# A transformer block's setup reordered: transfers in another order, filler matmuls, some work moved between engines

## The chip, the core and the metric

One core of a Trainium2 chip runs the whole program. Its engines are named as in the profile: PE (TensorE: matmuls, and PEld its weight loads), DVE (VectorE), ACT (ScalarE), POOL (GpSimd), SP (SyncE, which only issues transfers here). The metric is the device time of one execution in microseconds (us); lower is better. Everything stays in float32: a product in which accuracy matters is made of three matmuls on a high and a low part of each operand (names ending in _hi and _lo).

## What is computed

Eight sequences of 256 tokens with 256 features pass an attention block and a mixture-of-experts block, both modulated by a condition vector per sequence:

```python
mod = (silu(c) @ wmod).reshape(8, 6, 1, 256)
sa, ca, ga, sb, cb, gb = (mod[:, i] for i in range(6))
ga, gb = bounded(ga), bounded(gb)        # sign kept, size at least 0.25
h = layernorm(x) * (1 + ca) + sa
x = x + ga * attention(h, W_pack, W_o, conv_k, conv_v)
h = layernorm(x) * (1 + cb) + sb
x = x + gb * experts(h)                  # 32 experts, top 4, and a shared one
```

attention: qkv = h @ W_pack gives 16 query heads and 8 key and value heads of 128 features; q and k are rotated (x * cos + swapped x * sin), k and v pass a causal convolution of two taps per head; scores have a causal window of 128; the heads' outputs go through W_o.

## The kernel before

**Tiles and stages.** The batch is worked in four pairs of sequences (512 tokens). For a pair, h is held transposed (features on partitions) in two chunks c of 128 features, each as hT_hi and hT_lo. A projection project(m) makes one head of 128 features for the 512 tokens: six matmuls of 512 columns into one of two PSUM banks PJ (two chunks times hi*hi, hi*lo, lo*hi). The heads of a group come as k, q, v, q (head_of). 128 steps n of attention units follow (32 a pair), each with scores, softmax, a transpose of the probabilities, the weighted values and the output product; projections run four steps ahead (LEAD), so a prologue of four steps does project(0) to project(3) and nothing else. After the 128 steps come the shared expert and the 32 experts.

**Order.** It is written out by hand: each engine has its own program, `for n in STEPS` with the same step numbers, and the engines meet in semaphores. Hooks in the first pair's steps do further setup: W_STEPS and WO_STEPS split the later weight chunks and W_o into hi and lo parts (w_high, wo_high on ACT; w_low, wo_low on DVE a step later), MOD_STEPS compute the rest of the modulation.

**The setup, engine by engine.** SP (lines 343 to 373) issues in this order: c, ident, the first pair's rows xin (512 KB, line 347), the first third of the modulation weights wm (512 KB, line 349), the eight chunks wraw of W_pack (512 KB each, line 352, in W_ORDER), W_o as one transfer (2,048 KB, line 359), the rest of wm (1,024 KB), and next_x(1), the second pair's rows, which waits for the first pair's transposes (line 365); then the router's weights and the clearing of slot_rows. ACT (from line 482) issues cosT and sinT, computes silu(c) (L488), then issues mask, tri, ebase, wnorm, cwk and cwv (L494): eight small tables that share the semaphore ld_const.

PE (from line 1328): waits for silu and ident, transposes silu(c) (L1342) into bank U0, waits for DVE's copy scT and for wm, and computes the four 128-feature pieces of scale and shift with 16 matmul instructions of 8 columns (L1348) into U1. It then waits for modT and transposes the normalised rows (L1357, four a chunk, into U0 and U1). DVE: statistics of xin as soon as it has landed (L934, L937), the normalisation in place (L945), modT (L919, L920), the lo parts of weight chunks 0 and 1 (w_low, L1007), then hT_lo of both chunks (L951), then w_low of the third. ACT: rstd (L499, L500), w_high of chunks 0 and 1 (L578), then for each c the scaling hst (prepare_h, L508, two operations) and hT_hi (prepare_hi, L515), then w_high of the third. Weight chunks beyond these three (W_FIRST) are split in W_STEPS.

**Rotation of a projected head** (project and rope): ACT copies the halves swapped from PJ into qsw (L532, L533), DVE multiplies PJ by cosT (L965), POOL multiplies qsw by sinT (L768) and adds (L772); rope_done counts the sums. Then for k: ACT's tap (L540) and DVE's convolution kc (L970). The first scores (L1387, L1388) need kc and the first rotated q.

The waits that the change touches: ACT, DVE and POOL wait for all eight tables before their first steps, PE before step 0; PE waits for W_o before step 3; project(0) waits for both h_lo_done and, as every projection of the first pair, for w_lo_done.

```python
pe.wait_ge(modt_done, 1)          # before the transposes, line 1351
...
if l == 0:
    pe.wait_ge(h_lo_done, HC * (p + 1))
...
if p == 0:
    pe.wait_ge(w_lo_done, w_chunks(l))
```

## Time and profile before

| what | value |
|---|---|
| median of 3 runs | 765.53 us (765.27 to 766.3) |
| the profiled execution | 769.37 us, its span 766.9 us |
| PE / DVE / ACT / POOL busy | 731.1 / 531.6 / 467.7 / 425.5 us |
| mean granted PE clock | 0.990 |
| transferred | 84.42 MB, mean 110 GB/s |

Busy time is the sum over an engine's instructions; the span runs from the first to the last of them, and the execution's own time lies 2.5 us above it. The page divides the span into 40 slices of 19 us. In the first, PE is busy three tenths and in the second eight; from the fourth to the twenty-seventh it is busy nine tenths or more. Transfers are at eight to nine tenths of their engines in the first two slices and then mostly low.

### The profile page before, as it was taken

What the parts mean: (1) busy time and instruction counts of PE and PEld (TensorE: products, weight loads), DVE (VectorE), ACT (ScalarE), POOL (GpSimd) and SP (SyncE); (2) the same over time, 40 slices, a digit from 0 to 9 for tenths busy, and PEclk for the clock granted to TensorE, in tenths of its full rate; (3) what the DMA queues carried; (4) which work ended last, traced back from release to release, by engine and by line L of the source; (5) the groups of instructions that cost most, each with busy time, mean ns of one, the idle gap of its engine ahead of it and who ended that gap; (6) DMA issues with size and microseconds to landing.
All of it is one profiled execution on the core that took longest, in us unless ns stands there. A gap on an engine that the chain in (4) does not pass through costs nothing.

```text
span 766.9 us, 12813 instructions
## 1 busy us (share of the span) xinstructions
PE 731.1 (95%) x4114; PEld 620.8 (81%) x4114; DVE 531.6 (69%) x1552; ACT 467.7 (61%) x1277; POOL 425.5 (55%) x337
## 2 busy tenths in 40 slices
PE   3899999999999999999999999999988999999997
PEld 3688889998899898889989888989866767777775
DVE  4598788679877768987776797778665215564373
ACT  5688878777886677788667777877554212222110
POOL 0644445554466488646647875654534517468356
PEclk9999999999999999999999999999999999999999
DMA  8960005800005011100401101040359689996772
GB/s 294 322 136 1 2 1 175 287 1 2 1 1 168 26 40 48 40 1 1 158 8 40 46 28 62 16 165 1 123 145 237 191 289 272 282 240 74 163 233 82
DMA packets 62353, 84.42 MB, mean 110 GB/s; under 512 B 6312, under 2 KB 50229, under 8 KB 62288
## 3 DMA queue, kind: packets, MB, share of 16 engines
q1 hardware_dynamic: 51440, 70.56, 29.8%
q0 software_dynamic: 7680, 8.95, 6.2%
q10 hardware_dynamic: 3168, 4.11, 1.5%
q8 instruction: 33, 0.54, 0.3%
q14 instruction: 32, 0.26, 0.1%
HBM read 54.81 MB, written 33.51 MB: 115 GB/s over the span
## 4 chain that ended last, share of the span: by engine, by line
PE 76%; DVE 11%; ACT 6%; DMA 2%; issue 2%; POOL 1%; SPq 0%; ACTq 0%; POOLq 0%
PE PJ L1335 22%; PE OUT L1443 9%; PE U L1428 6%; PE U L1388 6%; PE U L1593 5%; PE U L1417 4%; PE U L1387 3%; PE U L1429 3%; PE U L1335 3%; PE OUT L1539 3%; PE U L1539 2%; PE XB L1612 2%; PE OUT L1612 2%; PE XB L1335 2%; ACT U L546 1%
## 5 line engine op out<-in xcount | busy, mean ns | idle before, releaser
L768 POOL TENSOR_TENSOR qsw<-qsw,sinT 128x512 f32<-128x512 f32 x96 | 126.2, 1314 | 184.6 <-ACT qsw L533 183.7
L977 DVE CUSTOM_DVE_ANT_0 U<-U,mask 128x128 f32<-128x128 f32 (+1 forms) x256 | 86.6, 379 | 54.8 <-PE U L1388 54.4
L546 ACT ACTIVATE U<-U,nmax 128x128 f32<-128x128 f32 (+1 forms) x256 | 100.4, 392 | 32.2 <-DVE nmax L977 31.7
L1335 PE MATMUL PJ<-hT_hi,w_hi 128*128 128x512 f32 x256 | 113.8, 445 | 4.0 <-DVE hT_lo L951 3.7
L1335 PE MATMUL PJ<-hT_lo,w_hi 128*128 128x512 f32 x256 | 103.5, 404 | 0.0
L1335 PE MATMUL PJ<-hT_hi,w_lo 128*128 128x512 f32 x256 | 103.1, 403 | 0.0
L772 POOL TENSOR_TENSOR qr<-qr,qsw 128x512 f32<-128x512 f32 x64 | 82.5, 1289 | 31.3 <-DVE qr L965 30.8
L532 ACT ACTIVATE qsw<-PJ 64x512 f32<-64x512 f32 x96 | 57.0, 594 | 58.1 <-PE PJ L1335 49.3
L779 POOL DMA_INDIRECT slot_rows<-xn,sidx x64 | 64.4, 1006 | 45.6 <-issue 12.0
L1443 PE MATMUL OUT<-wo_hi,oT_hi 128*128 128x256 f32 x256 | 83.0, 324 | 1.4 <-DVE wo_lo L1001 1.2
L994 DVE TENSOR_TENSOR oT_lo<-U,oT_hi 128x256 fp32r<-128x256 f32 x128 | 54.1, 423 | 41.2 <-ACT oT_hi L553 41.0
L1428 PE MATMUL U<-pT,vN 128*128 128x256 f32 x256 | 77.7, 385 | 1.8 <-ACT pT L566 1.1
L1388 PE MATMUL U<-kc,qr 128*128 128x256 f32 x256 | 77.4, 385 | 0.0
L987 DVE TENSOR_TENSOR prob<-U,rinv 128x384 f32<-128x384 f32 x128 | 71.4, 558 | 4.4
L1443 PE MATMUL OUT<-wo_hi,oT_lo 128*128 128x256 f32 x256 | 72.7, 284 | 0.0
L553 ACT ACTIVATE oT_hi<-U 128x256 fp32r<-128x256 f32 x128 | 49.3, 385 | 38.0 <-PE U L1429 30.8
L862 POOL DMA_INDIRECT expert_sum<-ye,slot_token x32 | 49.7, 1552 | 39.6 <-DVE ye L1276 23.2
L1443 PE MATMUL OUT<-wo_lo,oT_hi 128*128 128x256 f32 x256 | 71.6, 280 | 0.0
L1387 PEld LDWEIGHTS U<-kc,qr 128*128 128x128 f32 x256 | 47.5, 192 | 25.2 <-DVE oT_lo L994 7.9
L566 ACT ACTIVATE pT<-U 128x384 f32<-128x384 f32 x128 | 63.3, 495 | 0.7 <-PE U L1417 0.7
L1417 PE MATMUL U<-ident,prob 128*128 128x128 f32 x384 | 63.0, 273 | 0.2 <-DVE prob L987 0.2
L1335 PEld LDWEIGHTS PJ<-hT_hi,w_hi 128*128 128x128 f32 x256 | 49.5, 193 | 13.2 <-DVE hT_lo L951 4.1
(212 smaller groups left out, 1827.6 us busy)
## 6 DMA issues: line engine op xcount, KB each, us to landing
wgu<-in_dram SPq DMA_DIRECT2D x32, 352.0 KB, 9.4
expert_sum<-blank SPq DMA_DIRECT2D x3, 2176.0 KB, 17.8
slot_rows<-blank SPq DMA_DIRECT2D x1, 4624.0 KB, 26.3
late_sums<-expert_sum SPq DMA_DIRECT2D x9, 512.0 KB, 8.9
wd_a<-in_dram SPq DMA_DIRECT2D x12, 352.0 KB
wraw<-in_dram SPq DMA_DIRECT2D x8, 512.0 KB, 11.5
bcm<-mod_rows SPq DMA_DIRECT2D x8, 512.0 KB, 6.8
xe<-slot_rows ACTq DMA_DIRECT2D x10, 289.0 KB, 6.3
```

The lines of the kernel that those rows point to most:

```text
L546: last = act.activation(U[n % 3][:, a:z], U[n % 3][:, a:z], ACT.Exp, scale=-1.0, bias=nmax[:, n % 4, j:j + 1], accum_out=rsum[:, n % 4, j: ...
L768: pool.tensor_tensor(pair3(qsw[:, n % NQSW, :]), pair3(qsw[:, n % NQSW, :]), both(sinT[:, :]), ALU.mult).then_inc(t2_done, 1)
L772: pool.tensor_tensor(rope_buffer(m), rope_buffer(m), qsw[:, n % NQSW, :], ALU.add).then_inc(rope_done, 1)
L779: pool.indirect_dma_start(out=slots_d, out_offset=bass.IndirectOffsetOnAxis(ap=sidx[:, c:c + 1], axis=0), in_=xn[:, p % 2, c // TOPK, :], ...
L977: last = dve.tensor_tensor_reduce(out=U[n % 3][:, a:z], in0=U[n % 3][:, a:z], in1=allowed, scale=-float(HD) ** -0.5, scalar=3.4e38, op0=AL ...
L987: dve.tensor_tensor(prob[:, n % 2, :].rearrange("p (j k) -> p j k", k=PN), U[n % 3][:, 0:3 * PN].rearrange("p (j k) -> p j k", k=PN), rinv ...
L1335: last = pe.matmul(out_ap, a(c), b_(c), start=(n == 0), stop=(n == len(steps) - 1))
L1387: pe.matmul(U[n % 3][:, 0:PN], q[:, 0:PN], k[:, 0:PN], start=True, stop=True)
L1388: pe.matmul(U[n % 3][:, PN:3 * PN], q[:, PN:S], k, start=True, stop=True).then_inc(sc_ps, 1)
L1417: last = pe.transpose(U[n % 3][:, j * PN:(j + 1) * PN], prob[:, n % 2, j * PN:(j + 1) * PN], ident[:, :])
L1428: pe.matmul(o, v[:, 0:PN], pT[:, n % 2, 0:S], start=True, stop=False)
L1443: last = pe.matmul(OUT[b][:, t * H:(t + 1) * H], o, w[:, head, :], start=(head == 0 and t == 0 and i == 0), stop=(head == NH - 1 and i == ...
```

## The change

One commit changes the setup and nothing behind the first pair's steps:

- **Transfers.** ident and the first third of wm move to the head of ACT's queue. The first rows come in two halves, each with its own semaphore. The eight tables move from ACT's queue to SP's: cosT, sinT, cwk and cwv (semaphore ld_rope) behind the third weight chunk; mask, tri, ebase and wnorm (ld_const) behind the fourth. W_o comes in four parts: part 0 behind these, part 1 behind the second pair's rows, parts 2 and 3 behind the last chunk. The second pair's rows come behind the seventh chunk; the rest of wm comes last.
- **PE.** Fifteen filler matmuls (spin: ident by ident into OUT0, whose content is never read): 3 before the transposes of silu(c), 2 behind them, 5 behind the wm matmuls, 5 behind the transposes of x. The transposes no longer wait for modT, since the small products now lie in XB and U2. Head 0 has an order of its own: first the products with hT_hi of both chunks, then those with hT_lo.
- **Between engines.** The scaling of chunk 1 goes from ACT to DVE (first_h), the lo parts of the first two weight chunks from DVE to POOL, and the sine product and sum of head 0 from POOL to DVE. On ACT hT_hi of chunk 1 comes right behind that of chunk 0.
- **Waits.** Each engine waits for ld_rope before its first steps and for ld_const where the mask (DVE, step 0) or tri (PE, step 32) is first read; ACT waits for the part of W_o that it splits; ht_used counts one less.

The diff, cut:

```diff
@@ sync
-            sp.dma_start(ident[:, :], ident_t).then_inc(ld_ident, 16)
-            sp.dma_start(xin[:, :, :], x_pair(0)).then_inc(ld_xin, 16)
             wm_src = wmod.rearrange("(c p) n -> p c n", p=PN)
-            sp.dma_start(wm[:, :, 0:2 * H], wm_src[:, :, 0:2 * H]).then_inc(ld_wm, 16)
+            for b in range(2):
+                sp.dma_start(xin[:, 2 * b:2 * b + 2, :],
+                             x[b * S:(b + 1) * S, :].rearrange("(t p) h -> p t h", p=PN)).then_inc(ld_first[b], 16)
...
             for j in W_ORDER[:W_FIRST]:
                 w_load(j)
-            for j in W_ORDER[W_FIRST:]:
-                w_load(j)
-            sp.dma_start(wo[:, :, :], w_o.rearrange("(n p) h -> p n h", p=PN)).then_inc(ld_wo, 16)
-            sp.dma_start(wm[:, :, 2 * H:6 * H], wm_src[:, :, 2 * H:6 * H]).then_inc(ld_wmr, 16)
+            for dst, src in ((cosT[:, :], cos_t), (sinT[:, :], sin_t),
+                             (cwk[:, :], conv_k.rearrange("g t -> (g t)").partition_broadcast(PN)),
+                             (cwv[:, :], conv_v.rearrange("g t -> (g t)").partition_broadcast(PN))):
+                sp.dma_start(dst, src).then_inc(ld_rope, 16)
+            w_load(W_ORDER[W_FIRST])
+            for dst, src in ((mask[:, :], mask_t[:, PN:3 * PN]), (tri[:, :], tri_t), (ebase[:, :], ebase_t),
+                             (wnorm[:, :], w_norm.partition_broadcast(PN))):
+                sp.dma_start(dst, src).then_inc(ld_const, 16)
...
+            wo_load(0)
+            for j in W_ORDER[W_FIRST + 1:W_FIRST + 4]:
+                w_load(j)
             next_x(1)
+            wo_load(1)
+            w_load(W_ORDER[W_FIRST + 4])
+            wo_load(2)
+            wo_load(3)
+            sp.dma_start(wm[:, :, 2 * H:6 * H], wm_src[:, :, 2 * H:6 * H]).then_inc(ld_wmr, 16)
@@ scalar
-            act.dma_start(cosT[:, :], cos_t).then_inc(ld_const, 16)
-            act.dma_start(sinT[:, :], sin_t).then_inc(ld_const, 16)
+            act.dma_start(ident[:, :], ident_t).then_inc(ld_ident, 16)
+            act.dma_start(wm[:, :, 0:2 * H], wmod.rearrange("(c p) n -> p c n", p=PN)[:, :, 0:2 * H]).then_inc(ld_wm, 16)
...
-            for c in range(HC):
-                prepare_h(0, c, U[c])
-                prepare_hi(0, c)
+            prepare_h(0, 0, U[0])
+            prepare_hi(0, 0)
+            prepare_hi(0, 1)
             w_high(W_FIRST - 1)
...
-            act.wait_ge(ld_const, 128)
+            act.wait_ge(ld_rope, 64)
@@ gpsimd
-            pool.wait_ge(ld_const, 128)
+            for n in range(W_FIRST - 1):
+                j = W_ORDER[n]
+                pool.wait_ge(w_hi_done, n + 1)
+                pool.tensor_tensor(w_lo[j][:, :, :], wraw[j][:, :, :], w_hi[j][:, :, :].bitcast(F32),
+                                   ALU.subtract).then_inc(w_lo_first, 1)
+            pool.wait_ge(ld_rope, 64)
@@ vector, in project(m)
+                if m == 0:
+                    own(dve.tensor_tensor(pair3(qsw[:, 0, :]), pair3(qsw[:, 0, :]), both(sinT[:, :]), ALU.mult))
+                    dve.tensor_tensor(rope_buffer(0), rope_buffer(0), qsw[:, 0, :], ALU.add).then_inc(rope_done, 1)
@@ vector
+            def first_h(c):
+                dve.wait_ge(ht_ps, c + 1)
+                dve.wait_ge(modt_done, 1)
+                for b in range(2):
+                    last = dve.tensor_scalar(hst[:, 0, c, b * S:(b + 1) * S], U[c][:, b * S:(b + 1) * S], modT[:, 2 + c, b:b + 1],
+                                             modT[:, c, b:b + 1], ALU.mult, ALU.add)
+                last.then_inc(first_h1, 1)
...
             mod_features()
-            for n in range(W_FIRST - 1):
-                w_low(n)
+            first_h(1)
             for c in range(HC):
                 prepare_lo(0, c)
             w_low(W_FIRST - 1)
             dve.wait_ge(fills, 10)
-            dve.wait_ge(ld_const, 128)
+            dve.wait_ge(ld_rope, 64)
@@ tensor
+            def spin(n):
+                for _ in range(n):
+                    pe.matmul(OUT[0][:, 0:PN], ident[:, :], ident[:, :], start=True, stop=True)
+            pe.wait_ge(ld_ident, 16)
+            spin(SPINS[0])
             pe.wait_ge(silu_done, 1)
...
+            def first_head(high, low, cols):
+                for c in range(HC):
+                    pe.wait_ge(h_hi_done, c + 1)
+                    pe.matmul(PJ[0][:, :], high[:, c, cols], hT_hi[:, 0, c, :], start=(c == 0), stop=False)
+                    if c == 0:
+                        pe.wait_ge(w_lo_first, 1)
+                    pe.matmul(PJ[0][:, :], low[:, c, cols], hT_hi[:, 0, c, :], start=False, stop=False)
+                for c in range(HC):
+                    pe.wait_ge(h_lo_done, c + 1)
+                    last = pe.matmul(PJ[0][:, :], high[:, c, cols], hT_lo[:, 0, c, :], start=False, stop=(c == HC - 1))
+                last.then_inc(pj_ps, 1)
```

## Rows read from the trace of the kernel before

**Rows 1.** The page: busy time of each engine; the chain that ended last.

```profile
PE 731.1 (95%) x4114; PEld 620.8 (81%) x4114; DVE 531.6 (69%) x1552; ACT 467.7 (61%) x1277; POOL 425.5 (55%) x337
...
PE 76%; DVE 11%; ACT 6%; DMA 2%; issue 2%; POOL 1%; SPq 0%; ACTq 0%; POOLq 0%
```

**Rows 2.** Windows: us, PE, PEld, DVE, ACT, POOL busy (instructions), PEclk, DMA share, GB/s.

```profile
44.00:540.00 496.00, 489.90 (x3012) 434.54 (x3011) 397.39 (x1223) 380.27 (x1072) 289.93 (x231) 0.99 0.16 54
```

**Rows 3.** Timeline, 0 to 22 us: start, us, engine, line, operation, tiles, idle before.

```profile
3.55 0.35 PE L1342 MATMUL U<-ident,sc 8*128 8x8 f32 x2 [3.55 <-DMA ident<-in_dram]
...
6.13 0.75 DVE L934 BATCH_NORM_STATS2 st<-xin 128x6 f32<-128x256 f32 x2 [2.02 <-DMA xin<-in_dram]
...
8.60 1.38 DVE L945 TENSOR_SCALAR xin<-xin,mv,rstd 128x256 f32<-128x256 f32 x4 [0.51 <-ACT rstd L500]
...
8.67 3.55 PE L1348 MATMUL U<-scT,wm 128*128 128x8 f32 x16 [4.76 <-DMA wm<-in_dram]
...
10.48 1.06 ACT L578 ACTIVATE w_hi<-wraw 128x1024 fp32r<-128x1024 f32 x1 [1.92 <-DMA wraw<-in_dram]
...
12.57 1.97 PE L1357 MATMUL U<-ident,xin 128*128 128x128 f32 x8 [0.35 <-DVE modT L920]
...
13.10 1.06 ACT L578 ACTIVATE w_hi<-wraw 128x1024 fp32r<-128x1024 f32 x1 [1.57 <-DMA wraw<-in_dram]
14.19 1.02 ACT L508 ACTIVATE hst<-U,modT 128x256 f32<-128x256 f32 x2
...
15.24 0.63 ACT L515 ACTIVATE hT_hi<-hst 128x512 fp32r<-128x512 f32 x1
...
17.47 0.69 DVE L951 TENSOR_TENSOR hT_lo<-hst,hT_hi 128x512 fp32r<-128x512 f32 x1 [0.88 <-ACT hT_hi L515]
...
18.41 1.23 DVE L1007 TENSOR_TENSOR w_lo<-wraw,w_hi 128x1024 fp32r<-128x1024 f32 x1 [0.25 <-ACT w_hi L578]
```

**Rows 4.** Timeline, 21 to 50 us, same columns.

```profile
22.59 0.69 DVE L965 TENSOR_TENSOR kr<-PJ,cosT 128x512 f32<-128x512 f32 x1 [2.95 <-ACT qsw L533]
22.61 1.28 POOL L768 TENSOR_TENSOR qsw<-qsw,sinT 128x512 f32<-128x512 f32 x1 [20.43 <-ACT qsw L533]
...
23.74 0.59 ACT L532 ACTIVATE qsw<-PJ 64x512 f32<-64x512 f32 x1 [1.29 <-PE PJ L1335]
...
24.32 0.40 PE L1335 MATMUL PJ<-hT_hi,w_lo 128*128 128x512 f32 x1
...
24.55 0.39 PE L1335 MATMUL PJ<-hT_hi,w_hi 128*128 128x512 f32 x1
...
26.57 1.60 POOL L772 TENSOR_TENSOR qr<-qr,qsw 128x512 f32<-128x512 f32 x1
...
28.31 0.46 PE L1387 MATMUL U<-kc,qr 128*128 128x128 f32 x2 [0.91 <-POOL qr L772]
...
31.75 0.74 DVE L934 BATCH_NORM_STATS2 st<-xin 128x6 f32<-128x256 f32 x2
...
35.11 1.28 POOL L772 TENSOR_TENSOR kr<-kr,qsw 128x512 f32<-128x512 f32 x1
35.29 2.18 DVE L1007 TENSOR_TENSOR w_lo<-wraw,w_hi 128x1024 fp32r<-128x1024 f32 x1
```

**Rows 5.** The chain of waits, 17 to 22 us: start, us, what.

```profile
18.22 2.94 PE PJ L1335 x6
```

**Rows 6.** Windows of the opening, columns as in rows 2.

```profile
0.00:6.00 6.00, 0.35 (x2) 0.28 (x2) 0.17 (x1) 2.98 (x3) 1.55 (x14) 1.00 0.65 188
10.00:12.00 2.00, 2.00 (x11) 2.00 (x10) 0.00 (x0) 1.06 (x1) 0.00 (x0) 1.00 0.51 150
12.00:20.00 8.00, 3.97 (x14) 3.19 (x14) 5.22 (x7) 5.19 (x8) 0.00 (x0) 1.00 1.02 377
```

**Rows 7.** Transfers issued from 0 to 8 us: KB each, us from issue to landing.

```profile
wm<-in_dram SPq DMA_DIRECT2D x1, 512.0 KB, 6.4
...
cwv<-in_dram ACTq DMA_DIRECT2D x1, 8.0 KB, 8.7
```

More of the change, by code:

```diff
@@ L239, in adaln_block @@
         ld_c, ld_ident, ld_wm, ld_xin, ld_xres, ld_bcm = sem("ld_c"), sem("ld_ident"), sem("ld_wm"), sem("ld_xin"), sem("ld_xres"), sem("ld_bcm")
-        ld_wmr, ld_const, ld_wr, ld_wo = sem("ld_wmr"), sem("ld_const"), sem("ld_wr"), sem("ld_wo")
+        ld_first = [sem("ld_first0"), sem("ld_first1")]
+        first_h1, w_lo_first = sem("first_h1"), sem("w_lo_first")
+        ld_wmr, ld_const, ld_rope, ld_wr = sem("ld_wmr"), sem("ld_const"), sem("ld_rope"), sem("ld_wr")
+        ld_wo = [sem(f"ld_wo{j}") for j in range(4)]
         ld_w = [sem(f"ld_w{j}") for j in range(8)]
@@ L317, in pair3, with ht_scaled @@
             return ap.rearrange("p (b s) -> p b s", b=2)
+        def ht_scaled(p, c):
+            return HC * p + c + (p == 0)
         def rope_number(m):
@@ L489, in _ @@
             act.preload_act_table_set("natural_log_exp_and_others")
-            for dst, src in ((mask[:, :], mask_t[:, PN:3 * PN]), (tri[:, :], tri_t),
-                             (ebase[:, :], ebase_t), (wnorm[:, :], w_norm.partition_broadcast(PN)),
-                             (cwk[:, :], conv_k.rearrange("g t -> (g t)").partition_broadcast(PN)),
-                             (cwv[:, :], conv_v.rearrange("g t -> (g t)").partition_broadcast(PN))):
-                act.dma_start(dst, src).then_inc(ld_const, 16)
             def prepare_norm(p):
@@ L930, in prepare_stats @@
             def prepare_stats(p, b):
-                if b == 0:
-                    dve.wait_ge(ld_xin, 16 * (p + 1))
+                if p == 0:
+                    dve.wait_ge(ld_first[b], 16)
+                elif b == 0:
+                    dve.wait_ge(ld_xin, 16 * p)
                 for t in range(2 * b, 2 * b + 2):
@@ L964, in project @@
                     return
-                dve.tensor_tensor(pair3(rope_buffer(m)), pair3(PJ[m % 2][:, :]), both(cosT[:, :]), ALU.mult).then_inc(pj_dve, 1)
+                last = dve.tensor_tensor(pair3(rope_buffer(m)), pair3(PJ[m % 2][:, :]), both(cosT[:, :]), ALU.mult)
+                last.then_inc(pj_dve, 1)
+                if m == 0:
+                    own(dve.tensor_tensor(pair3(qsw[:, 0, :]), pair3(qsw[:, 0, :]), both(sinT[:, :]), ALU.mult))
+                    dve.tensor_tensor(rope_buffer(0), rope_buffer(0), qsw[:, 0, :], ALU.add).then_inc(rope_done, 1)
             def k_conv(G):
@@ L1336, in halves @@
                 return last
+            def spin(n):
[3 more added lines that the diff above has]
+            spin(SPINS[0])
             pe.wait_ge(silu_done, 1)
-            pe.wait_ge(ld_ident, 16)
             for c in range(HC):
-                last = pe.transpose(U[0][:, c * B:(c + 1) * B], sc[:, c * PN:(c + 1) * PN], ident[0:B, 0:B])
+                last = pe.transpose(XB[:, c * B:(c + 1) * B], sc[:, c * PN:(c + 1) * PN], ident[0:B, 0:B])
             last.then_inc(sct_ps, 1)
+            spin(SPINS[1])
             pe.wait_ge(sct_done, 1)
@@ L1347, in _ @@
                 for c in range(HC):
-                    last = pe.matmul(U[1][:, k * B:(k + 1) * B], wm[:, c, k * PN:(k + 1) * PN], scT[:, c, :],
+                    last = pe.matmul(U[2][:, k * B:(k + 1) * B], wm[:, c, k * PN:(k + 1) * PN], scT[:, c, :],
                                      start=(c == 0), stop=(c == HC - 1))
             last.then_inc(modt_ps, 1)
-            pe.wait_ge(modt_done, 1)
+            spin(SPINS[2])
             def prepare_t(p, c, bank):
@@ L1363, in project @@
                 cols = slice(at, at + HD)
-                if l == 0:
+                if l == 0 and p > 0:
                     pe.wait_ge(h_lo_done, HC * (p + 1))
@@ L1369, in project @@
                     pe.wait_ge(pj_dve, m - 1)
+                if m == 0:
+                    first_head(w_hi[j], w_lo[j], cols)
+                    return
                 if p == 0:
-                    pe.wait_ge(w_lo_done, w_chunks(l))
+                    if w_chunks(l) < W_FIRST:
+                        pe.wait_ge(w_lo_first, w_chunks(l))
+                    else:
+                        pe.wait_ge(w_lo_done, w_chunks(l) - W_FIRST + 1)
                 halves(PJ[m % 2][:, :], HC,
@@ L1506, in _ @@
                 prepare_t(0, c, U[c])
+            spin(SPINS[3])
             def mod_rows(j):
```

31 lines of the change are left out of this document (18 added, 13 removed).

## The prediction

> **What bounds the kernel now.** I read the page first: TensorE (PE) is busy 95% of the span and carries 76% of the chain that ended last [rows 1]. Then the stages: between 44 and 540 us PE is busy 489.9 of 496 us [rows 2]. Whatever shortens the setup therefore reaches the end one for one, as long as the first attention steps, where the other engines still set the pace, keep their form; it can't be won twice there. The opening must be read instruction by instruction. It goes thus [rows 3]: the modulation weights wm are what PE waits for until 8.67; 16 small matmuls take 3.55; only after modT does PE transpose x (12.57); h is scaled and split on ScalarE (ACT) from 14.19 and on VectorE (DVE) until 18.16; head 0 starts at 18.22. From there [rows 4, 5]: PJ0 is ready at 21.16; its ACT copies, two GpSimd (POOL) operations of head 0, then two of head 1 come one after another, until the first scores at 28.31.
>
> 0.2% of 765.53 is 1.53 us, about what a measurement here can tell from nothing. The profiled execution took 769.37 with a span of 766.9, so it is 3.84 above the median; I work in its times and take the difference off the median.
>
> **Modulation weights first.** x, wm, ident and c are 1,096 KB, 1.12 MB. The old kernel had moved 188 GB/s x 6 us = 1.13 MB by 6.0 [rows 6], but with 256 KB of tables in it, and wm behind x. Now wm is issued at about 1.16, where sinT stood, and shares the engines with x. Bounds: 6.0 (all four moved, no lag), and 1.16 + 6.4 = 7.6 (its old time from issue to landing [rows 7]). Lag counts, since x, with 0.86 MB up to it, was seen only at 6.13; I take 6.8. ident is issued 0.5 us earlier and lands near 3.0. The x halves gain about a half's work on DVE: old x-hat took 6.13 to 9.98, the new ends near 9.3. That is hidden: wm sets the pace.
>
> **Filler matmuls.** Three spins stand before the transposes of silu(c): 1.3 us from 3.0, so these go at 4.3, not 3.55; two more end near 5.4. All of it is covered by the wait for wm; without that cover it would cost 2.2. A spin is a float32 matmul by ident; the nearest row is L1348, 3.55/8 = 0.44 us each, with the same loads; the floor is a transpose of the same size, 0.25. The wm matmuls go 6.85 to 10.4, modT is there at 10.75, behind five spins that end at 12.6; the transposes end at 14.6. So far nothing is gained: the old ones ran 12.57 to 14.54. The five spins have eaten the 1.8 us of wm, for DVE's modT hides only 0.35 of their 2.2.
>
> **From the transposes to head 0.** Old: 14.54 to 18.22. ACT was late then (hst at 14.19, for it was copying a weight chunk), and did both halves serially. New: U0 is full at 13.6; hst 1.02 and hi 0.64 end at 15.35; DVE does h1 meanwhile, 14.6 to 15.4 (two operations; the SBUF form in rows 3 is 0.345 each, a PSUM read may be dearer, so 0.7 to 1.0); hi of it 16.05; the lo parts, 0.70 each, 16.1 and 16.8. Five more spins end at 16.75, beside all of this. Head 0's new order needs the lo parts last. It starts at 16.8, 1.4 earlier.
>
> **The weight chunks' lo parts.** Moved from DVE to POOL: 128x512 takes 1.28 there [rows 4], so 2.56 each. The chunks can't land later than the old 10.48 and 13.10 [rows 3], since less stands ahead of them; POOL is then done by 13.1 + 1.06 + 2.56 = 16.7 at the worst, and by 15.2 if they land 1.5 us earlier. Needed at 17 and 18.3: hidden, no cost. w_high(2) moves behind hT_hi of both parts and ends near 17.1, w_low(2) near 18.3, needed for head 2 at 20: hidden.
>
> **The clock.** The profile's column says 1.00 throughout the opening, but six projection matmuls take 2.94 [rows 5], some 0.45 apart, and the last of head 1 stand 0.23 apart from 24.32 [rows 4]: the lower level (1.2 GHz), then the upper (2.4). It had risen 6 us after PE began head 0, its first long stretch of wide matmuls; the 3.6 us of 8-column matmuls and the transposes before hadn't raised it. The same 6 us counted from the five spins at 10.4 give 16.4. So head 0 runs at the upper level: 6 x 0.23 + 0.2 = 1.55, PJ0 at 18.35 (old 21.16, gain 2.8), PJ1 at 19.75 (old 23.7, gain 4.0).
>
> **Head 0's rotation on DVE.** ACT's copies take 1.2 each, to 19.6 and 20.95. DVE: three operations of 0.69 for head 0 (the cosine product, the sine product, the sum) for the old 0.69 beside POOL's 2 x 1.28, so 21.7. POOL starts head 1 at 21.0 instead of behind head 0's two (22.61 + 2.6 = 25.2). Both now want SBUF: a DVE w_lo, 1.23 by itself [rows 3], took 2.18 where a POOL operation of 1.28 had begun 0.18 before it, and one POOL sum took 1.60 for 1.28 [rows 4]. I add 1.0 in all (bounds 0, and 1.9 for a delay of 0.95 on either engine): qr's product ends about 22.9, POOL's sum 24.4, k's tap and convolution, about 0.7 each behind 21.7 and this delay, by 24.5. The first scores start at 24.7, against 28.31: 3.6 us sooner. The Trainium skill, page SBUF — State Buffer, section SBUF: two separate sides, holds that the pair shared by VectorE and GpSimd is an exclusive lock, the loser blocked for the whole instruction; w_lo agrees, ending 1.08 after POOL's end against 1.22 by the rule. By that rule, if each engine once waits out a whole operation of the other (1.28 and 0.69), the scores would start at 25.6 instead of 24.7, and the time would be 762.8.
>
> **The transfers behind.** wo goes in four parts, the second x between the chunks: behind 5.9 MB (seven chunks of 512 KB, a quarter of wo, the tables, the first x and wm) where 8.9 stood; old DVE statistics ran at 31.75 with no wait [rows 4]. 3.0 MB at 377 GB/s [rows 6] are 7.9 us, so it lands near 24, and is needed at 28. cos, sin and both conv tables now stand on SP's queue behind chunk 2: issued near 5, the old cwv took 8.7 to land [rows 7], so 14 to 16, needed at 19.6. mask and tri are needed at 25. The wait at step 3 for wo and the wo_hi of step 1 find the first part long there. Cost nothing, while that slack lasts. Steps 0 to 3 are otherwise the same work, with the same DVE stalls, so the 3.6 stays.
>
> Sum: 1.4 (start of head 0) + 1.4 (its clock) + 1.2 (head 1 at that clock) - 0.4 (net of moving head 0's rotation, with the contention) = 3.6. 765.53 - 3.6 = 761.9.
>
> **Rivals.**
> 1. The clock rises early, within the spins or transposes (6 us counted from 6.85 give 12.9). Then transposes and second spins go at the upper level, 1 us each, less what ACT doesn't follow: 1.7 more, 760.2. For: PE now idles little from 6.85. Against: the x8 matmuls did not raise it before. Chance 0.22.
> 2. It rises only after head 0, as before some 6 us into wide matmuls: head 0 costs 2.9, head 1 about 2: 1.5 back, 763.4. For: the transposes may count for little. Chance 0.10.
> 3. wm isn't much earlier. At 7.6 the path moves 0.8 (762.7), at the old 8.5 it moves 1.7 (763.6); with a late clock too it would be no change. The Trainium skill, page DMA: Bandwidth & Descriptors, section Issuing engines are not separate DMA queues, says that issuing from several engines saves only the issue time; by that the gain is the 0.93 us between the issues, and the sum would be 762.7. For: x, wm and ident still share one set of engines, which moved 188 GB/s on average in that stretch. Against: 256 KB of tables leave their front, and wm no longer stands behind x. By the trace of before the rule can't be told, for wm was on one queue only. 0.12.
> 4. Slower: the small tables jam SP's queue. At 10 to 12 us the rate was 150 GB/s, between stretches of 377 [rows 6], while cwk and cwv, whose rows have only 64 bytes, were due. Now they stand before chunk 3 and, worse, before the wait of ACT, POOL and DVE for the tables. From a landing at 19.6 each us costs one; from 23.2 on the gain is gone, past 24.7 the kernel is measurably slower; 25.5 would give 767.8. It needs 20 us from issue where 8.7 was the most. 0.03.
> 5. The saving is lost again in steps 0 to 3, in DVE's long operations: 765.5. 0.03.
>
> The forecast itself has 0.50, its own range 760.6 to 763.2 (wm 6.0 to 7.6, contention 0 to 1.9). With rivals 1 to 3 the range is 759.7 to 764.2. Faster: 0.50 + 0.22 + 0.08 + 0.08 = 0.88; same 0.09; slower 0.03.
>
> **What would show it.** PE's first L1348 near 6.9, not 8.67; transposes not much before 12.5; head 0 near 16.8 with its matmuls 0.23 apart; three DVE operations for kr; first scores near 24.7; the lead of 3.6 us still there when PE's unbroken stretch begins. I am wrong if head 0's matmuls are 0.43 apart, if wm is waited for until after 7.6, or if the scores' lead is not found again at the end.

## The result and the profile after

| | before | changed |
|---|---|---|
| median, 13 executions each | 764.73 us | 760.77 us |
| lowest | 762.36 us | 758.73 us |
| profiled execution: span, mean granted clock | 766.9 us, 0.990 | 756.9 us, 0.994 |

The ratio is 0.9939 (95% interval 0.992 to 0.9958): faster by 0.61%, 4.0 us between the medians, where 3.6 were forecast. The changed kernel was measured once more beside the last experiments: 758.99 against 765.29, ratio 0.9908 (0.9877 to 0.994). One of the changed kernel's 13 executions (831.9), and one of the third run's ten below (830.6), took far longer, at a lower granted clock, and are left out of the ratios.

The page of the changed kernel, against [rows 1]:

```profile
span 756.9 us, 12875 instructions
...
PE 731.7 (97%) x4144; PEld 622.0 (82%) x4144; DVE 530.8 (70%) x1554; ACT 466.7 (62%) x1275; POOL 428.5 (57%) x337
```

PE's busy time is 731.7 against 731.1, with 30 instructions more (a filler is two); what went is time in which it waited. The opening, in the timeline (columns as in rows 3), against [rows 3, 4]:

```profile
1.16 0.45 ACTq L509 DMA_DIRECT2D wm<-in_dram  x1
...
6.02 0.75 DVE L961 BATCH_NORM_STATS2 st<-xin 128x6 f32<-128x256 f32 x2 [1.26 <-DMA xin<-in_dram]
...
6.33 3.55 PE L1396 MATMUL U<-scT,wm 128*128 128x8 f32 x16 [0.63 <-DMA wm<-in_dram]
...
8.49 3.51 DVE L972 TENSOR_SCALAR xin<-xin,mv,rstd 128x256 f32<-128x256 f32 x4 [0.51 <-ACT rstd L518]
...
9.48 4.72 POOL L851 TENSOR_TENSOR w_lo<-wraw,w_hi 128x1024 fp32r<-128x1024 f32 x2 [7.30 <-ACT w_hi L598]
...
9.73 2.48 PE L1383 MATMUL OUT<-ident 128*128 128x128 f32 x10
...
12.05 1.97 PE L1405 MATMUL U<-ident,xin 128*128 128x128 f32 x8
...
13.81 1.56 PE L1383 MATMUL OUT<-ident 128*128 128x128 f32 x10
...
15.12 0.48 PE L1412 MATMUL PJ<-hT_hi,w_hi 128*128 128x512 f32 x1
...
15.44 0.40 PE L1415 MATMUL PJ<-hT_hi,w_lo 128*128 128x512 f32 x1
...
17.12 0.59 ACT L553 ACTIVATE qsw<-PJ 64x512 f32<-64x512 f32 x1 [0.45 <-PE PJ L1418]
...
18.45 0.60 ACT L553 ACTIVATE qsw<-PJ 64x512 f32<-64x512 f32 x1
...
19.77 0.69 DVE L996 TENSOR_TENSOR kr<-kr,qsw 128x512 f32<-128x512 f32 x1
...
19.79 1.82 POOL L788 TENSOR_TENSOR qsw<-qsw,sinT 128x512 f32<-128x512 f32 x1 [5.58 <-ACT qsw L554]
...
21.25 0.90 DVE L1001 SCALAR_TENSOR_TENSOR kc<-kr,cwk,k 128x512 f32<-128x512 f32 x1 [0.19 <-ACT k L561]
...
21.69 1.61 POOL L792 TENSOR_TENSOR qr<-qr,qsw 128x512 f32<-128x512 f32 x1
...
23.44 0.46 PE L1454 MATMUL U<-kc,qr 128*128 128x128 f32 x2 [0.65 <-POOL qr L792]
```

The reader is to see five things. PE's wait for wm ends at 6.33 instead of 8.67. The 16 small matmuls and five fillers (L1383) then follow without a gap, and the transposes (L1405) start at 12.05, only 0.5 before the old ones. The last ten filler instructions take 1.56 where those before the transposes took 2.48: the clock has risen between 13.8 and 15, from the lower level (1.2 GHz) to the upper (2.4 GHz). Head 0 starts at 15.12 instead of 18.22, with its first two matmuls already 0.32 apart (0.59 before). The first scores come at 23.44 instead of 28.31.

One row was not expected: DVE's normalisation of the rows took 3.51 us instead of 1.38. GpSimd's first w_low runs from 9.48 to 11.85 beside it. The view of that one line (min/median/max in ns) shows a single operation held up:

```profile
L972 DVE TENSOR_SCALAR xin<-xin,mv,rstd x16: 401/408/2537, 8.5 to 324.2; 128x256 f32<-128x256 f32 x16
```

One of the 16 took 2,537 ns against a median of 408, and it ended 0.15 after GpSimd's first operation.

The lead was then followed step by step. Two scores matmuls of the kernel before (steps 52 and 56), and the same two of the changed one:

```profile
239.24 0.46 PE L1387 MATMUL U<-kc,qr 128*128 128x128 f32 x2
...
259.54 0.38 PE L1387 MATMUL U<-kc,qr 128*128 128x128 f32 x2
```

```profile
234.48 0.46 PE L1454 MATMUL U<-kc,qr 128*128 128x128 f32 x2
...
253.15 0.38 PE L1454 MATMUL U<-kc,qr 128*128 128x128 f32 x2
```

28.31 - 23.44 = 4.87 at step 0, 4.75 at step 4 (44.15 against 39.40), 4.76 at step 52, and 259.54 - 253.15 = 6.39 at step 56. From step 4 to step 52 the lead stays between 4.72 and 4.83. It then grew three times by 1.5 to 1.6, at steps 54, 86 and 118, to 9.52 at the last step. None of that comes from the opening. Windows of 10 us of the kernel before (columns as in rows 2) hold one stretch each at half the clock; the windows of the same steps in the changed kernel (one is shown) don't, but it had such stretches further on, at 568 to 584:

```profile
246.00:256.00 10.00, 10.00 (x59) 8.95 (x58) 5.06 (x23) 4.66 (x15) 4.09 (x4) 0.83 0.47 169
379.00:389.00 10.00, 10.00 (x63) 9.19 (x62) 4.85 (x18) 4.64 (x16) 3.93 (x4) 0.83 0.46 144
512.00:522.00 10.00, 10.00 (x61) 9.10 (x61) 5.37 (x19) 5.35 (x17) 4.20 (x4) 0.83 0.40 135
```

```profile
241.30:251.30 10.00, 10.00 (x70) 9.26 (x71) 6.57 (x33) 5.22 (x16) 4.07 (x4) 1.00 0.45 159
568.00:584.00 16.00, 14.88 (x65) 11.60 (x66) 8.51 (x35) 5.81 (x10) 7.08 (x6) 0.79 0.98 258
```

PEclk is 0.83 against 1.00, PE being busy for all of the 10 us in both. The three lie 32 steps apart, which is one pair: each comes where PE ends the router's 24 matmuls of 34 columns. In the kernel before:

```profile
245.79 0.26 PE L1335 MATMUL XB<-wr_hi,xnT_hi 128*128 128x34 f32 x1
...
248.36 0.26 PE L1335 MATMUL XB<-wr_hi,xnT_lo 128*128 128x34 f32 x1
...
249.89 0.63 PE L1335 MATMUL PJ<-hT_hi,w_lo 128*128 128x512 f32 x1
```

They stand 0.11 apart, and the projection matmul at 249.89 already takes the 0.63 of the lower level. In the fourteen profiles of this case the clock falls 19 times between 44 and 540 us, each time between 0.5 before and 1.0 after the end of these 24; in the other 23 passages it stays up. No run left them out, so that they are the cause is not shown.

Each stretch costs 1.6 us, and how many an execution has changes from one to the next, in both kernels: of the changed kernel's executions, those with a mean clock of 0.994 took 758.7 to 759.6, one with 0.990 took 764.5. So the two spans (10.0 apart) overstate the change, and ratios of ten executions, whose intervals here reach 1.5 to 2.3 us to either side, can't settle the parts of the change. What the setup brings is read from the steps: 4.76 us. The experiments below are therefore read by the start of head 0, the first scores and the scores of step 4, and by the time only where it speaks.

### The profile page after: what moved, and what is told of

Read it like the earlier page. It is cut to its first block, busy times and chain, and to the rows that moved or that the text cites. A ratio compares the mean times of both kernels' runs of the same rounds, so it can differ in the third digit from the quotient of the medians.

```text
span 756.9 us, 12875 instructions
## 1 busy us (share of the span) xinstructions
PE 731.7 (97%) x4144; PEld 622.0 (82%) x4144; DVE 530.8 (70%) x1554; ACT 466.7 (62%) x1275; POOL 428.5 (57%) x337
## 4 chain that ended last, share of the span: by engine, by line
PE 80%; DVE 11%; ACT 5%; issue 2%; DMA 1%; POOL 0%; ACTq 0%; DVEq 0%; POOLq 0%
PE PJ L1376 22%; PE OUT L1510 9%; PE U L1495 6%; PE U L1455 6%; PE U L1658 5%; PE U L1484 4%; PE OUT L1607 3%; PE U L1607 3%; PE U L1454 3%; PE U L1496 3%; PE U L1376 3%; PE OUT L1677 2%; PE XB L1677 2%; PE XB L1376 2%; ACT U L567 1%
## 5 line engine op out<-in xcount | busy, mean ns | idle before, releaser
L1376 PE MATMUL PJ<-hT_hi,w_hi 128*128 128x512 f32 x254 | 110.8, 436 | 1.1 <-issue 1.1
L1376 PE MATMUL PJ<-hT_lo,w_hi 128*128 128x512 f32 x254 | 100.4, 395 | 0.0
L1376 PE MATMUL PJ<-hT_hi,w_lo 128*128 128x512 f32 x254 | 100.1, 394 | 0.0
L1454 PEld LDWEIGHTS U<-kc,qr 128*128 128x128 f32 x256 | 46.5, 188 | 24.7 <-DVE oT_lo L1025 9.2
L1454 PE MATMUL U<-kc,qr 128*128 128x128 f32 x256 | 50.8, 280 | 7.9 <-DVE oT_lo L1025 4.2
```

The costliest lines, as they stand in the source:

```text
L1376: last = pe.matmul(out_ap, a(c), b_(c), start=(n == 0), stop=(n == len(steps) - 1))
L1454: pe.matmul(U[n % 3][:, 0:PN], q[:, 0:PN], k[:, 0:PN], start=True, stop=True)
```

## The experiments

Twelve runs: ten other kernels, then the fifth and the changed one once more. Each ratio is against the kernel before, measured beside that run. In the changed kernel head 0 starts at 15.1, the first scores at 23.4, step 4 at 39.4; in the kernel before 18.2, 28.3 and 44.2.

### Without the fillers

```diff
-        SPINS = (3, 2, 5, 5)
+        SPINS = (0, 0, 0, 0)
```

> The changed kernel without its fifteen filler matmuls, all else kept. In the changed kernel the transposes of x start at 12.05, head 0 at 15.10, the first scores at 23.44 and those of step 4 at 39.40 (before: 12.57, 18.22, 28.31, 44.15). My theory (the fillers cost 2 us in front of the transposes and are paid back by the clock): transposes at 10.2 and at the lower level, head 0 near 13.3, its matmuls 0.43 apart and those of head 1 too; PJ0 full near 16.1 (17.1 with fillers), PJ1 near 18.7 (18.4), first scores at 23.4 to 23.9, so within 0.5 us of the changed kernel. Rival A (the clock needs the fillers; without them PE's short pieces keep it low): PE stays at the lower level through heads 0 to 3, first scores at 24.5 or later, step 4 at 40.5 or later. Rival B (the fillers are a cost only): the clock rises at the same moment near 13.8, first scores near 21.8, step 4 near 37.8.

```profile
6.90 3.55 PE L1396 MATMUL U<-scT,wm 128*128 128x8 f32 x16 [3.06 <-DMA wm<-in_dram]
...
9.03 3.50 DVE L972 TENSOR_SCALAR xin<-xin,mv,rstd 128x256 f32<-128x256 f32 x4 [0.51 <-ACT rstd L518]
...
12.58 1.97 PE L1405 MATMUL U<-ident,xin 128*128 128x128 f32 x8 [2.13 <-DVE xin L972]
...
19.96 0.63 PE L1376 MATMUL PJ<-hT_lo,w_hi 128*128 128x512 f32 x1
...
20.39 0.63 PE L1376 MATMUL PJ<-hT_hi,w_lo 128*128 128x512 f32 x1
```

First scores at 25.51, step 4 at 41.46; median 762.61, ratio 0.9953 (0.9929 to 0.9978). Rival A is right in its times: without the fillers all of head 0 and most of head 1 run at the lower level (19.96 to 20.39 is 0.43 for one matmul), though not heads 2 and 3, and 2.1 us are lost in step 4. My theory's two effects don't balance, for a reason that was not in it: without fillers the transposes did not start at 10.2 but at 12.58. They waited for DVE's normalisation, held up by GpSimd. So the fillers behind wm cost nothing in the changed kernel; two things of the same length stand side by side there. (wm and the rows both were ready some 0.55 later in this execution than in the changed kernel's, which accounts for the 12.58 against 12.05; so of the 2.1 us the fillers' own part is some 1.6.)

### wm back on SP's queue

```diff
             (SP) both halves of xin
+            sp.dma_start(wm[:, :, 0:2 * H], wm_src[:, :, 0:2 * H]).then_inc(ld_wm, 16)
             (SP) chunks
...
-            act.dma_start(wm[:, :, 0:2 * H], ...).then_inc(ld_wm, 16)
```

> The changed kernel with the first third of wm back on SP's queue, behind both halves of the first rows and in front of the chunks; ident stays first on ScalarE's. In the changed kernel PE's wm matmuls start at 6.33, before at 8.67. My theory (the place in the stream of transfers decides, since the tables no longer stand in front and two queues share the engines): wm is waited for until 7.0 to 7.6, everything behind it moves by 0.7 to 1.3 one for one, first scores 24.1 to 24.7. Rival A (a second queue saves only the issue time, 0.9 us, which the removed ident and tables give back anyway): within 0.3 us of 6.33, first scores 23.4 to 23.7. Rival B (the queue decides it all): back at 8.5, first scores 25.6.

```profile
2.16 0.47 SPq L359 DMA_DIRECT2D wm<-in_dram  x1
...
4.64 0.74 DVE L962 BATCH_NORM_STATS2 st<-xin 128x6 f32<-128x256 f32 x2
...
8.81 3.56 PE L1397 MATMUL U<-scT,wm 128*128 128x8 f32 x16 [3.15 <-DMA wm<-in_dram]
```

wm was issued 1.0 later (2.16 against 1.16) and waited for until 8.81, 2.5 later: the place behind the rows on SP's queue decides it all (rival B), though ident had left that queue's front and the tables ScalarE's; my own 7.0 to 7.6 missed. First scores 25.66, step 4 41.61; ratio 0.9976 (0.9957 to 0.9996). 2.2 us of the 4.76 hang on this one transfer. The rows pay for it: their first half was used from 4.64 here and from 6.02 in the changed kernel. The rule of the Trainium skill, page DMA: Bandwidth & Descriptors, section Issuing engines are not separate DMA queues, that only issue time is saved, is not borne out for the transfer itself: 1.0 us of issue against 2.5 us of landing. That both queues share one set of engines is borne out, by what the rows paid.

### Head 0's rotation back on GpSimd

```diff
-                if m % 4 == 2 or m == 0:
+                if m % 4 == 2:
...
-                if m == 0:
-                    own(dve.tensor_tensor(pair3(qsw[:, 0, :]), ..., both(sinT[:, :]), ALU.mult))
-                    dve.tensor_tensor(rope_buffer(0), rope_buffer(0), qsw[:, 0, :], ALU.add).then_inc(rope_done, 1)
```

> The changed kernel with head 0's sine product and sum back on GpSimd. My theory: kr is ready at 18.45 + 1.28 + 1.28 = 21.0 instead of 20.46, head 1's two follow it on GpSimd, 21.0 to 23.6 with one operation delayed by 0.3, so the first scores start near 23.9 to 24.1 instead of 23.44: 0.5 to 0.7 us of the change come from here. In the prediction the move was worth 2.6 - 0.7 - 1.0 of contention, near 0.8. Rival (the contention of the two engines eats all of it): first scores at 23.3 to 23.5.

First scores 24.08, step 4 40.06; ratio 0.9948 (0.9922 to 0.9974). 0.66 us in step 4, inside my theory's 0.5 to 0.7, and the rival is out. (0.13 of it lies ahead of head 0, which started at 15.25.) PE was idle from 22.19 to 24.08 here, where the changed kernel had 0.65 of idle time, and the clock then fell for a while:

```profile
25.50:28.90 3.40, 3.40 (x11) 2.64 (x10) 2.56 (x9) 2.96 (x7) 1.28 (x1) 0.50 1.07 387
```

The scores of step 1 came 1.6 later than in the changed kernel (27.61 against 26.01), those of step 3 only 0.66 (34.36 against 33.70): PE's idle times between them, 1.6 together in the changed kernel, had shrunk to 0.4 and took up the loss.

### The lo parts of two chunks back on VectorE

```diff
@@ vector
             mod_features()
+            for n in range(W_FIRST - 1):
+                j = W_ORDER[n]
+                dve.wait_ge(w_hi_done, n + 1)
+                dve.tensor_tensor(w_lo[j][:, :, :], ...).then_inc(w_lo_first, 1)
             first_h(1)
```

and the same four lines taken from GpSimd's program.

> The changed kernel with the lo parts of the first two weight chunks back on VectorE, behind modT and before h of chunk 1. In the changed kernel VectorE's normalisation of the first rows took 3.51 us instead of 1.38, beside GpSimd's two operations (9.48 to 14.20). My theory: on VectorE they take 1.23 each from 12.2, so VectorE comes to h1 at 14.7 instead of 14.06 and the normalisation is back at 1.4: h1 moves by 0.6, hT_hi and hT_lo of chunk 1 too, head 0's last matmuls with them, first scores 23.9 to 24.1. Rival A (the move to GpSimd costs through the shared access what it saves): first scores 23.3 to 23.5. Rival B (the normalisation, not the fillers, sets the transposes' start): transposes earlier than 12.0, first scores before 23.2.

```profile
8.49 1.38 DVE L967 TENSOR_SCALAR xin<-xin,mv,rstd 128x256 f32<-128x256 f32 x4 [0.51 <-ACT rstd L518]
...
9.74 2.48 PE L1383 MATMUL OUT<-ident 128*128 128x128 f32 x10
...
12.01 1.92 PE L1405 MATMUL U<-ident,xin 128*128 128x128 f32 x8
```

First scores 23.35, step 4 39.31; ratio 0.9946 (0.9923 to 0.997). The normalisation is back at 1.38, yet the transposes still start at 12.01, now behind the fillers. Rival A is right in its number: the move to GpSimd brings nothing here. My own expectation, 0.5 later, missed: head 0 started at 15.07. Rival B, by itself, is out.

### Both covers of the transposes removed

```diff
-        SPINS = (3, 2, 5, 5)
+        SPINS = (3, 2, 0, 5)
```

on top of the last kernel.

> Two things taken off the transposes' start at once: lo parts of the first two chunks on VectorE (so that its normalisation takes 1.38 again and ends near 9.9) and no fillers behind the wm matmuls (3, 2, 0, 5). Neither alone moved the start of the transposes from 12.0 to 12.6. Theory (two covers of the same length, the fillers until 12.0 and the slowed normalisation until 12.0): the transposes start at 10.2 to 10.4, right behind modT, h of both chunks is ready near 13.5, the five fillers end near 14.5 at the lower level, head 0 starts near 14.5 instead of 15.1. What follows depends on the clock: if it rises by 14.5, first scores near 22.9; if it needs 6 us from the transposes, heads 0 and 1 run partly at the lower level and first scores are at 23.5 to 24.5. Rival (modT or something else still holds the transposes): start at 11.5 or later.

```profile
9.72 1.97 PE L1405 MATMUL U<-ident,xin 128*128 128x128 f32 x8
...
11.48 1.79 PE L1383 MATMUL OUT<-ident 128*128 128x128 f32 x10
...
13.03 0.48 PE L1412 MATMUL PJ<-hT_hi,w_hi 128*128 128x512 f32 x1
```

The transposes start at 9.72, behind the small matmuls, head 0 at 13.03 and already at the upper level; first scores 21.53, step 4 37.49, 1.9 us ahead of the changed kernel. That confirms the two parallel covers: taking away either alone did not move the transposes, taking away both moved them by 2.3. All of it came earlier than my 10.2 and 14.5, and the clock rose before head 0. The median, 761.75 (ratio 0.9946, 0.9918 to 0.9975), does not show it; see the repeat below.

### Fillers by groups

```diff
-        SPINS = (3, 2, 5, 5)
+        SPINS = (3, 2, 5, 0)
```

> The changed kernel without the last five fillers (those between the transposes and head 0). If the clock needs an unbroken stretch up to head 0: PE idles 14.0 to 15.1, head 0 and part of head 1 at the lower level, first scores 24.3 to 25.5. If the five behind the wm matmuls and the transposes suffice: the clock rises near 14 all the same and the first scores are at 23.3 to 23.6. Step 4 follows with the same distance (changed kernel 39.40).

```diff
-        SPINS = (3, 2, 5, 5)
+        SPINS = (0, 0, 5, 5)
```

> The changed kernel without the first five fillers (before and behind the transposes of silu(c)), the ten later ones kept. Theory: they end at 5.4, a second of idle and 3.55 us of 8-column matmuls follow, so they do nothing: first scores 23.2 to 23.7, as with them. Rival: they raise the clock for later; without them it rises after 15.5 and the first scores come at 24.3 or later.

Without the last five: head 0 at 14.82, first scores 23.09, step 4 39.03; in that execution the clock rose during the transposes (1.52 for the eight) and did not fall again, though PE was idle for 1.40 before head 0. Without the first five: head 0 at 15.39, first scores 23.62, step 4 39.56, with wm awaited until 6.55. Each was profiled once. So the first five do nothing that could be seen, and with the clock risen by then the last five aren't needed; whether they are in an execution in which it rises later was not seen.

### The second pair's rows last

```diff
-            wo_load(0)
-            for j in W_ORDER[W_FIRST + 1:W_FIRST + 4]:
+            for j in W_ORDER[W_FIRST + 1:W_FIRST + 5]:
                 w_load(j)
-            next_x(1)
-            wo_load(1)
-            w_load(W_ORDER[W_FIRST + 4])
-            wo_load(2)
-            wo_load(3)
+            for j in range(4):
+                wo_load(j)
             sp.dma_start(wm[:, :, 2 * H:6 * H], ...).then_inc(ld_wmr, 16)
+            next_x(1)
```

> The changed kernel with W_o and the second pair's rows back in the old order: all chunks, W_o (in its four parts), the rest of wm, then the rows. Theory (the new order gains nothing itself but protects the 4.8 us): the opening is that of the changed kernel, first scores 23.4; the rows land at about 30 to 32 as before, and VectorE, which wants them at 27.0, waits for 3 to 4.7 us in step 0; PE's step 4 comes at 42.5 to 44 instead of 39.4, and the time is within 0.2% of the kernel before. Rival (the transfers run far enough ahead by themselves, now that nothing holds the queue up): rows by 28, step 4 at 39.4 to 40.5, and the order was worth nothing.

In the changed kernel DVE comes to these rows at 27.00 and finds them there:

```profile
27.00 0.42 DVE L961 BATCH_NORM_STATS2 st<-xin 128x6 f32<-128x256 f32 x1
```

With the old order:

```profile
32.83 0.76 DVE L958 BATCH_NORM_STATS2 st<-xin 128x6 f32<-128x256 f32 x2 [5.96 <-DMA xin<-in_dram]
...
35.98 1.22 PE L1492 MATMUL U<-pT,vN 128*128 128x256 f32 x2 [6.46 <-ACT pT L583]
```

First scores 23.23, as fast as any; but DVE waits 5.96 us for the rows, PE's next matmuls wait 6.46, and step 4 comes at 45.13, later than in the kernel before. Median 766.92, ratio 1.0027 (0.9997 to 1.0057). All of the gain is gone. More is lost than my theory's 3 to 4.7 because the rows came at 32.83, later than the 30 to 32 I had reckoned with: against 27.00 that is already 5.8, and step 4 is 5.7 later. PE's clock also fell during that wait (mean granted clock 0.50 from 32 to 42 us); what that cost by itself was not separated. The reordering behind the first chunks gains nothing that its own place in the trace shows, and without it the rest is worth nothing.

### The transfers alone

The changed kernel with SPINS all 0 and everything computed as before: rotation on GpSimd, lo parts on VectorE, h of chunk 1 on ScalarE, head 0 in the common order.

```diff
-            prepare_h(0, 0, U[0])
-            prepare_hi(0, 0)
-            prepare_hi(0, 1)
+            for c in range(HC):
+                prepare_h(0, c, U[c])
+                prepare_hi(0, c)
```

> Of the change the transfers and their waits alone: wm and ident first on ScalarE's queue, rows in halves, tables and W_o between the chunks; no fillers, and chunk 1 of h, the lo parts, head 0's order and its rotation on the engines and in the order of the kernel before. Theory: wm is waited for until 6.3 (before 8.67), modT at 10.0, the normalisation takes 1.4 and ends near 9.9, so the transposes start at 10.2; VectorE's w_low of two chunks ends near 13.0, hT_lo of chunk 1 near 15.6, head 0 starts at 15.4 to 15.8 at the lower level and all the rest keeps the distance of before (10.1 to the first scores): first scores at 25.3 to 25.9, step 4 near 41.4: 2.7 of the 4.75 us. Rival (the parts need each other: without the work moved, the earlier wm is eaten by ScalarE's and VectorE's serial order): first scores 26.8 or later. If the clock rises earlier than 6 us into head 0, first scores 24.6.

```profile
8.44 1.38 DVE L964 TENSOR_SCALAR xin<-xin,mv,rstd 128x256 f32<-128x256 f32 x4 [0.51 <-ACT rstd L518]
...
9.87 1.97 PE L1397 MATMUL U<-ident,xin 128*128 128x128 f32 x8
...
11.09 1.02 ACT L526 ACTIVATE hst<-U,modT 128x256 f32<-128x256 f32 x2 [0.46 <-PE U L1397]
...
14.38 0.69 DVE L970 TENSOR_TENSOR hT_lo<-hst,hT_hi 128x512 fp32r<-128x512 f32 x1 [0.88 <-ACT hT_hi L533]
...
15.12 0.79 PE L1368 MATMUL PJ<-hT_hi,w_hi 128*128 128x512 f32 x1 [3.28 <-DVE hT_lo L970]
```

wm at 6.27, transposes at 9.87, head 0 at 15.12, as early as in the changed kernel but at the lower level: first scores 25.23, step 4 41.17, ratio 0.9961 (0.9938 to 0.9984). The transfers alone bring 2.98 of the 4.76. The work moved to other engines has not made head 0 earlier; from the transposes on it goes through ScalarE's serial chain here, 11.09 to 14.34 (there the second hT_hi ends), and takes as much time as the changed kernel spends in fillers.

### The fillers alone

The kernel before with the same fifteen fillers in the same places.

```diff
+            pe.wait_ge(ld_ident, 16)
+            spin(3)
             pe.wait_ge(silu_done, 1)
...
+            spin(2)
             pe.wait_ge(sct_done, 1)
...
+            spin(5)
             pe.wait_ge(modt_done, 1)
...
                 prepare_t(0, c, U[c])
+            spin(5)
```

> The kernel before with the same fifteen fillers in the same places (3 and 2 around the transposes of silu(c), 5 behind the wm matmuls, 5 behind the transposes of x) and nothing else. Theory: the five behind wm have no cover here (the normalisation ends at 9.98), so the transposes go from 12.57 to 14.4 and head 0 from 18.2 to 19.3 to 19.8; the clock is at the upper level by then, heads 0 and 1 take 1.4 each, PJ0 is full at 21.0 to 21.4 as before; GpSimd's chain behind it is unchanged: first scores 27.9 to 28.5, no gain. Rival (the clock alone is worth its 2 us): first scores 26.2 to 26.8.

First scores 29.79, step 4 45.63: 1.5 us slower than the kernel before (wm was waited for until 9.39 here, 0.7 of it). Both expectations missed. The transposes went to 15.07 as the theory says, but PE then stood idle from 18.4 to 20.26, ScalarE and DVE not being ready, and the clock, which had risen near 17.6, fell again near 21.0. The windows:

```profile
18.50:20.20 1.70, 0.00 (x0) 0.00 (x0) 0.82 (x2) 1.67 (x3) 0.00 (x0) 1.00 1.06 383
21.50:24.00 2.50, 2.50 (x7) 1.96 (x6) 0.19 (x1) 1.19 (x2) 0.00 (x0) 0.50 1.10 348
```

PE did nothing in the first; in the second it is busy throughout, at a granted clock of 0.50. Fillers that end before the work is ready were lost here. (One execution was profiled and timed, 765.14.)

### The faster opening, and the changed kernel, once more

> The version of the fifth run once more (lo parts of the first two chunks on VectorE, fillers 3, 2, 0, 5), against the changed kernel on the same chip. Its steps ran 1.9 us ahead of the changed kernel's, its median did not show it, and its ten executions had a mean clock of 0.989 to 0.993 where the changed kernel's had 0.990 to 0.995. Theory A (the shift of 1.9 us makes PE fall to the lower level for longer in the stage behind the attention steps, in most executions): the mean clock is again 0.989 to 0.993, and the median within 1 us of the changed kernel's. Theory B (chance): clocks like those of the changed kernel and a median 1.5 to 2.3 us below it. Step 4 at 37.2 to 37.9 in both.

> The changed kernel once more, on the same chip as the others of this set: first scores 23.1 to 23.7, step 4 at 39.0 to 39.7, median 3.5 to 4.8 us below the kernel before, mean clock 0.990 to 0.995.

The changed kernel: first scores 23.24, step 4 39.21, median 758.99, clocks 0.992 to 0.998. The other: step 4 38.42, median 760.88, ratio 0.9914 (0.9883 to 0.9944), clocks 0.990 to 0.994. Its step 4 was 1.0 ahead of the changed kernel's first profile and 0.8 of the repeat, not 1.9: the clock rose only when head 0 was nearly done. With the moment of the rise open by some 3 us, an earlier start can meet the lower level. The median doesn't show it as faster; rather the reverse, within the interval. So neither theory came out as written: step 4 missed both, and the median is 1.9 above the changed kernel's. In 16 of 16 executions its mean clock was 0.994 or less, in the changed kernel in 14 of 18, a difference that chance can make. In the profile of the fifth run it went through the stage behind the attention steps for long at the lower level:

```profile
568.00:590.00 22.00, 21.77 (x79) 16.37 (x80) 7.98 (x37) 4.74 (x9) 7.79 (x7) 0.69 0.92 264
```

```profile
568.00:590.00 22.00, 20.88 (x89) 15.79 (x90) 9.41 (x41) 7.36 (x13) 9.40 (x9) 0.84 0.95 269
```

0.69 over 22 us, where the changed kernel (the second row) had 0.84. In the repeat no such stretch lay there; three lay within the attention steps instead. Why it has more of them is open, and so is whether it beats the changed kernel.

## Why the prediction was right

**Forecast and mechanism held.** 761.9 was forecast, 3.6 us less; 760.77 was measured, 4.0 less (3.2 to 6.1 by the interval), and the steps show 4.76. That the medians came so near to 3.6 is in part luck: by the steps the sum was 1.2 short, in its first term by 1.7, with the second 0.4 too large. Each term of the sum, against the trace: start of head 0, 1.4 forecast, 3.1 measured (18.22 against 15.12); its clock 1.4, measured 1.0 (its ScalarE copy starts at 17.12 instead of 21.26, a lead of 4.1); head 1 at that clock 1.2, measured 1.2 (18.45 against 23.74, a lead of 5.3); rotation and contention -0.4, measured -0.4 (4.87 at the first scores). The mis-sized term is the first. In the second, head 0's matmuls waited for ScalarE's hT_hi and DVE's hT_lo, 0.37 and 0.20 as the trace puts it, so that it took 2.0 from its start to the copy, not 1.55.

**The start of head 0.** wm came at 6.33, not 6.8: 0.5. The clock rose near 14, not at 16.4, so the last five fillers took 1.6 instead of 2.15, and head 0, whose first matmuls need only the first chunk's hi part, began as they ended. I had hung head 0's start on 16.8, when the fillers and both lo parts would be done; the trace has the lo parts needed last, as I wrote, and waited for by 0.20 only. Rival 1, an early rise (760.2), was thus half right; rival 2, a rise behind head 0, came in no kernel that had both the new opening and fillers. In the ten profiles of kernels with fillers on the new opening the clock was up by the end of head 0 in all; counted from the first fillers behind wm or, where there are none, from the transposes, it rose 3 to 6 us after, so the 6 us of the prediction were the upper end.

**The step that failed without harm.** "The x halves gain about a half's work on DVE ... the new ends near 9.3. That is hidden: wm sets the pace." The rows became ready at 12.0, 2.7 later, because GpSimd's w_low held one DVE operation for 2.1 us. I had counted the contention in head 0's rotation and called the move of w_low free, looking only at when its result is needed and not at whom it blocks. It was hidden, though not by wm: by the five fillers, which I had booked as a cost of 2.2 on the path. The first, fourth and fifth run show that either of the two alone holds the transposes until 12.0 to 12.6, at least 2.3 us after the 9.72 of neither, and that the second beside the first costs nothing more.

**Contention.** I added 1.0 for both engines. GpSimd's sine product took 1.82 for 1.28 and its sum 1.61, 0.87 on the path. The Trainium skill's page SBUF — State Buffer, section SBUF: two separate sides, has an exclusive lock there: whichever engine starts first holds the shared pair of ports for its whole instruction. The trace agrees within 0.3: the normalisation was held until GpSimd's operation ended and was done 0.15 after (0.41 by the rule); GpSimd's product was held 0.54 where DVE's sum (19.77, 0.69) had 0.67 left, and its sum 0.33 where DVE's convolution (21.25, 0.90) had 0.46 left. What was too much is the prediction's use of the rule, a whole operation waited out on each engine, 1.9 in place of 0.87. Both its 24.7 and its 25.6 for the first scores were besides 1.3 too late at their start, since ScalarE's copies of head 0 ended at 18.31 instead of 19.6.

**Transfers.** The second rows, issued at 14.05, took 9.1 to land, near the reckoned 24, and were there at 27.00; the eighth run shows what the slack was worth. Rival 4, the jam of small tables, did not come: the four that the engines wait for first landed 6.9 to 7.3 us after issue on SP's queue. Rival 3 did not come: wm was used 2.3 earlier, and in the second run, issued 1.0 later and behind the rows, 2.5 later: its place among the transfers counts beside the issue time. Rival 5 did not come: from step 0 to step 4 the lead went from 4.87 to 4.75.

**What each part is worth**, in step 4, taken from the changed kernel: wm's queue 2.2, the fillers 1.6, head 0's rotation 0.7, the lo parts on GpSimd 0, the order of the late transfers 5.7. They don't add up to 4.76, and should not: the last is a cover, and the fillers brought only harm in the kernel before. The move of h1 to DVE and head 0's own order weren't tried one by one; with the transfers alone, without both, head 0 starts as early. Nor were ident's move, the rows in halves or W_o in parts taken by themselves.

## What to carry to other kernels

A transfer that the first real work waits for belongs near the head of a queue on which nothing large stands before it: a place behind the first rows cost 2.5 us here. Filler matmuls paid where they joined, without a gap, the last small work to the first large; in the kernel before, with 1.8 us of idle time behind them, they did only harm. Where they seem to cost, look whether something else holds the same gate. When the opening is made shorter, the next load can become the wall: follow each operand of the first steps to its landing before believing a lead, and read small gains in the steps of the trace, not in the spans.

## What the runs showed of the hardware

- A DVE operation on one SBUF tensor (128x256, 0.41 us) was held 2.1 us by a GpSimd operation with two SBUF operands, until that ended; GpSimd's operations were held 0.54 and 0.33 by DVE operations with 0.67 and 0.46 left.
- In the kernel before, PE's work from 8.67 to 14.5 (16 small matmuls, eight transposes) left the clock at the lower level (1.2 GHz), and it rose some 6 us after head 0 had begun. With fillers on the new opening it rose 3 to 6 us after the first behind wm (or the transposes). It fell again behind idle times of 1.8 us (the filler-only run) and 1.9 us (the third run), and within one of 6.5 us (the run with the rows last), but not behind one of 1.4 us (the sixth run). The profile's clock column reads 1.00 from the start of the opening, though the spacing of the matmuls (0.43, then 0.23) shows the lower level: it reports nothing before the first rise.
- PE, busy for 10 of 10 us, still has short stretches at the lower level that cost 1.6 us each. In the attention steps there were none to three of them in a profile, 19 in all, every one at the end of the router's 24 matmuls of 34 columns. Executions with a lower mean clock are the longer ones. Whether these matmuls bring the stretches was not tried.
